# Last normalisation behind the gelus, one mask as a clamped line on ScalarE, variances by fused sums: a change to an attention and product-key kernel

## What is computed

```
q = einsum('bne', x, w_q); mean, var over all tokens
q = (q - mean) * rsqrt(var + 1e-5) * gamma + beta
sim = einsum('pbnhd,hkpd->pbnhk', q, keys)        # 2 halves x 8 heads x 32 keys
sx, ix = top_k(sim[0], 8);  sy, iy = top_k(sim[1], 8)
all_scores = sx[:, None] + sy[None, :]            # 8 x 8 per head
scores, pk = top_k(all_scores, 8)
h = gelu_new(einsum('bnd,bnhkd->bnhk', x, down_embed[indices]))
h = softmax(scores) * h
out = einsum('bnhk,bnhkd->bnd', h, up_embed[indices])
x = layernorm(x + out)
```

## Time and profile before

| | |
|---|---|
| Median of 3 runs | 651.7 us (648.76 to 651.85) |
| The profiled execution | 650.28 us, span 648.5 us |
| VectorE (DVE) busy | 541.3 us, 83% of the span |
| TensorE (PE) busy | 520.1 us, 80% |
| ScalarE (ACT) busy | 410.9 us, 63% |
| GpSimd (POOL) busy | 402.2 us, 62% |
| TensorE's granted clock | tenths 6 to 9 between the 19th and 24th of 40 slices, 9 elsewhere |

### The profile page before, as it was taken

The page is one execution under the profiler, slowest core; times in us unless marked ns, Lnnn a source line. Parts: engine busy times, 40 slices in busy tenths (PEclk is TensorE's granted clock), DMA queues, the critical chain, the costliest instruction groups (busy, mean ns, idle before and its releaser), DMA issues.

```text
span 648.5 us, 42547 instructions
## 1 busy us (share of the span) xinstructions
PE 520.1 (80%) x17953; PEld 443.2 (68%) x17985; DVE 541.3 (83%) x1741; ACT 410.9 (63%) x813; POOL 402.2 (62%) x522
## 2 busy tenths in 40 slices
PE   0279999999998899994567888887787788778776
PEld 0158878888886577784346777776776777667676
DVE  5658989889897577864788889999999999999992
ACT  4246766677775557764164576677677668667764
POOL 8345546555552235442267768878878887887882
PEclk9989999999998999996667799999999999999999
DMA  6877975654516001000012223322332332233231
GB/s 201 246 221 233 285 206 172 188 191 148 195 56 226 17 18 33 17 1 5 5 45 54 66 48 81 77 61 64 77 76 49 81 77 58 68 77 76 50 77 44
DMA packets 45201, 64.39 MB, mean 99 GB/s; under 512 B 5488, under 2 KB 37360, under 8 KB 42608
## 3 DMA queue, kind: packets, MB, share of 16 engines
q1 hardware_dynamic: 45168, 63.97, 35.7%
HBM read 36.29 MB, written 8.65 MB: 69 GB/s over the span
## 4 chain that ended last, share of the span: by engine, by line
PE 40%; issue 17%; ACT 17%; POOL 12%; DVE 9%; DMA 3%; POOLq 1%; ACTq 1%; SPq 0%; another core or an unknown queue 0%; DVEq 0%
PE ps L754 8%; PE ps L813 5%; ACT early L1070 5%; PE ps L734 4%; ACT tile_rows L1082 4%; PE ps L769 4%; PE ps L826 4%; PE ps L744 3%; ACT L1070 3%; POOL tile_rows L663 3%; PE ps L919 3%; POOL rstd L690 2%; PE ps L780 2%; DMA xT<-terms 2%; PE ps L928 2%
## 5 line engine op out<-in xcount | busy, mean ns | idle before, releaser
L919 PE MATMUL ps<-arena,hid 128*32 128x32 f32 x8192 | 79.6, 200 | 53.8 <-DVE hid L1437 46.8
L919 PEld LDWEIGHTS ps<-arena,hid 128*32 128x32 f32 x8192 | 75.7, 112 | 60.0 <-issue 31.1
L968 ACT ACTIVATE arena<-ps 128x512 f32<-128x512 f32 x128 | 69.8, 595 | 54.3 <-PE ps L754 54.1
L928 PEld LDWEIGHTS ps<-xT,downT_sb 128*128 128x128 f32 x528 | 69.0, 204 | 13.5 <-issue 12.4
L1178 DVE TENSOR_REDUCE row_max<-ps 128x8 f32<-128x768 f32 x64 | 61.0, 953 | 17.5 <-PE ps L744 17.2
L928 PE MATMUL ps<-xT,downT_sb 128*128 (+1 forms) x528 | 68.7, 287 | 1.8 <-issue 0.2
L754 PE MATMUL ps<-ident,arena 128*128 128x128 f32 x512 | 69.3, 280 | 0.0
L940 PE MATMUL ps<-up_sb,prod 128*128 128x128 f32 x512 | 65.6, 282 | 0.3 <-DVE prod L1446 0.3
L1181 DVE TENSOR_TENSOR arena<-ps,row_max 128x768 f32<-128x768 f32 x64 | 61.3, 958 | 5.1 <-DVE row_max L1178 0.2
L669 POOL TENSOR_TENSOR wq_sb<-wq_sb,tile_rows 128x1024 f32<-128x1024 f32 x32 | 64.6, 2018 | 1.0 <-POOL tile_rows L663 0.4
L940 PEld LDWEIGHTS ps<-up_sb,prod 128*128 128x128 f32 x512 | 62.9, 196 | 0.5 <-DVE prod L1446 0.5
(11 more groups left out here) (161 smaller groups left out, 1332.5 us busy)
## 6 DMA issues: line engine op xcount, KB each, us to landing
arena<-r_x SPq DMA_DIRECT2D x128, 128.0 KB, 2.4
early<-terms SPq DMA_DIRECT2D x8, 720.0 KB
xT<-terms SPq DMA_DIRECT2D x8, 720.0 KB
hid<-terms SPq DMA_DIRECT2D x8, 720.0 KB
prod<-terms SPq DMA_DIRECT2D x8, 720.0 KB
x_pair<-in_x_wrapped SPq DMA_DIRECT2D x16, 256.0 KB, 4.5
xT_tile<-xT SPq DMA_DIRECT2D x34, 64.0 KB, 1.9
x<-in_x SPq DMA_DIRECT2D x8, 256.0 KB, 2.9
```

Source lines behind the costliest of these rows:

```text
L919: mm = nc.tensor.matmul(slots[32 * g:32 * g + 32, k, c], leftT[p][:, r // 2, r % 2, :], blocks_of[p][:, :, r // 2, r % 2, GROUP * g:GROUP ...
L928: mm = nc.tensor.matmul(ps[:, 4 + half, (c % 4) * P:(c % 4 + 1) * P], downT_sb[:, c * P:(c + 1) * P], xT[:, tok(t)].rearrange("p (q r k) - ...
L968: return nc.scalar.activation(out_ap, in_ap, ACT.Copy)
```

## The change

Three edits.

The first moves work on ScalarE. In `d_act` the limits are copied ahead of the exponentials, and `last_norm` of the older tile runs behind the gelus of tile t + 1 and the table load that follows them.

The second takes the fourth left mask from VectorE. Its comparison covers three masks, 128x256x3 elements instead of 128x1024. ScalarE's new `first_keys` writes the fourth as relu(1 + 2^110 * s): s is 0 for the largest key and negative for the others. VectorE's `masks` now waits for `firsts_done` where it waited for `relexp_done`, and POOL's `classes` waits for it too. `first_keys` itself waits until the left buffer has been transposed. In VectorE's order `normaliser` moves from ahead of the right mask to behind it.

The third replaces, for the variances, each product over three heads and each sum over them by one step for each head, which multiplies and writes the sum.

```diff
--- before.py
+++ after.py
@@ -49,6 +49,7 @@
 Q_SPLIT = (slice(0, 3 * QB), slice(3 * QB, PH))
 MASKED = -1e30
 SLACK = 2.0 ** -21
+STEEP = 2.0 ** 110
 TABLES = "natural_log_exp_and_others"
 
 
@@ -281,7 +282,6 @@
         r3_done = sem("r3_done")
         moment_ready = sem("moment_ready")
         z_banks = sem("z_banks")
-        prod_done = sem("prod_done")
         q_step = sem("q_step")
         q_var_done = sem("q_var_done")
         q_rstd_done = sem("q_rstd_done")
@@ -308,6 +308,7 @@
         limits_done = sem("limits_done")
         edges_done = sem("edges_done")
         masked = sem("masked")
+        firsts_done = sem("firsts_done")
         scaled = sem("scaled")
         right_ready = sem("right_ready")
         classes_done = sem("classes_done")
@@ -672,6 +673,7 @@
             def classes(t, p):
 
                 pool.wait_ge(masked, 2 * t + 2)
+                pool.wait_ge(firsts_done, t + 1)
                 hold(pool)
                 nc.gpsimd.tensor_tensor(left[p][:, :, :, 0:TERMS - 1], left[p][:, :, :, 0:TERMS - 1],
                                         left[p][:, :, :, 1:TERMS], ALU.subtract).then_inc(classes_done, 1)
@@ -1090,6 +1092,13 @@
                 copy(limits[p][:, :, 2:5:2].rearrange("p h a -> p a h"), top_rel[:, :, 1].rearrange("p (a h) -> p a h", a=2))
                 copy(limits[p][:, :, 7:10:2], stretch(top_rel[:, 0:PK_HEADS, 1:2], 2)).then_inc(limits_set, 1)
 
+            def first_keys(t, p):
+
+                need(a, leftT_done, t - 1)
+                nc.scalar.activation(left[p][:, :, :, TERMS - 1].rearrange("p i h -> p h i"),
+                                     ps[:, p, 0:PK_HEADS * KEYS].rearrange("p (h k) -> p h k", h=PK_HEADS), ACT.Relu,
+                                     bias=1.0, scale=STEEP).then_inc(firsts_done, 1)
+
             def last_mean(t, p):
 
                 a.wait_ge(up_done, t + 1)
@@ -1123,8 +1132,9 @@
                 for p in range(2):
                     t, o = 2 * i + p, 1 - p
                     if have(t + 1):
+                        set_limits(t + 1, o)
                         rel_exps(t + 1, o)
-                        set_limits(t + 1, o)
+                        first_keys(t + 1, o)
                     if have(t - 2):
                         last_mean(t - 2, p)
                     if have(t + 1):
@@ -1132,10 +1142,11 @@
                     if have(t - 2):
                         last_square(t - 2, p)
                         last_variance(t - 2)
-                        last_norm(t - 2, p, i - 1)
                     if have(t + 1):
                         gelus(t + 1, o)
                         a.preload_act_table_set(TABLES)
+                    if have(t - 2):
+                        last_norm(t - 2, p, i - 1)
             over_tiles(a, d_act)
 
 
@@ -1319,18 +1330,15 @@
                 v.wait_ge(z_banks, b + 1)
                 z3 = ps[:, b, 0:n * (P + 1)].rearrange("p (k c) -> p k c", c=P + 1)
                 V.tensor_copy(q_mean[:, QB * b:QB * b + n], z3[:, :, P])
-                V.tensor_tensor(prod[:, QB * b:QB * b + n, :], z3[:, :, 0:P], wqT_sb[:, QB * b:QB * b + n, :], ALU.mult
-                                ).then_inc(prod_done, 1)
-
-            def q_sums(b):
-                n = min(QB, PH - QB * b)
-                v.wait_ge(prod_done, b + 1)
-                return V.tensor_reduce(q_var[:, QB * b:QB * b + n], prod[:, QB * b:QB * b + n, :], AX_X, ALU.add)
-
+                for k in range(n):
+                    last = V.scalar_tensor_tensor(prod[:, QB * b + k, :], z3[:, k, 0:P], 1.0, wqT_sb[:, QB * b + k, :], ALU.mult,
+                                                  ALU.mult, accum_out=q_var[:, QB * b + k:QB * b + k + 1])
+                return last
 
             def q_variance(part):
 
                 ks = Q_SPLIT[part]
+                v.wait_ge(q_step, 3 * part + 1)
                 V.tensor_tensor(q_mean2[:, ks], q_mean[:, ks], q_mean[:, ks], ALU.mult).then_inc(q_step, 1)
                 v.wait_ge(q_step, 3 * part + 2)
                 V.tensor_tensor(q_var[:, ks], q_var[:, ks], q_mean2[:, ks], ALU.subtract).then_inc(q_step, 1)
@@ -1352,12 +1360,11 @@
                                 ).then_inc(keys_ready, 1)
 
             for b in range(6):
-                q_moments(b)
-                if b % 3:
-                    q_sums(b - 1)
+                last = q_moments(b)
                 if b % 3 == 2:
-                    q_sums(b).then_inc(q_step, 1)
+                    last.then_inc(q_step, 1)
                     q_variance(b // 3)
+
             def split_constants(part):
 
                 cols = slice(Q_SPLIT[part].start * KEYS, Q_SPLIT[part].stop * KEYS)
@@ -1418,11 +1425,13 @@
             def masks(t, p):
 
                 sims = ps[:, p, :].rearrange("p (a h k) -> p a k h", a=2, h=PK_HEADS)
-                v.wait_ge(relexp_done, t + 1)
+                v.wait_ge(firsts_done, t + 1)
                 V.tensor_tensor(right[p], bcast(sims[:, 1], 3, TERMS), bcast(limits[p][:, :, 3:7], 1, KEYS), ALU.is_ge
                                 ).then_inc(masked, 1)
+                normaliser(t, p)
                 v.wait_ge(edges_done, t + 1)
-                V.tensor_tensor(left[p], bcast(sims[:, 0], 3, TERMS), bcast(limits[p][:, :, 0:4], 1, KEYS), ALU.is_ge
+                V.tensor_tensor(left[p][:, :, :, 0:TERMS - 1], bcast(sims[:, 0], 3, TERMS - 1),
+                                bcast(limits[p][:, :, 0:TERMS - 1], 1, KEYS), ALU.is_ge
                                 ).then_inc(masked, 1)
 
             def turn_right(t, p, i):
@@ -1461,7 +1470,6 @@
                         gate(t - 1, o)
                     if have(t + 1):
                         edges(t + 1, o)
-                        normaliser(t + 1, o)
                         masks(t + 1, o)
                     if have(t):
                         turn_left(t, p)
```

## The result

The changed kernel takes 635.1 us (median of 4 runs, 633.6 to 637.8) beside 651.8 us for the kernel before, timed with it (median of 4, 648.8 to 654.4). The ratio is 0.9768, with a 95% interval of 0.9739 to 0.9797: 15.1 us faster, between 13.2 and 17.0. The profiled execution took 636.6 us, span 634.8, which is 13.7 less than the span of the kernel before.

A forecast was written before the change was run, and what follows sets the result against it. Bound in the steady last stage: VectorE's own work beside an equally long ScalarE-POOL-VectorE ring, plus 0.21 us wait. Terms 7.0 + 0.3 + 5.5 + 0.2 = 13.0 us off 650.28 or 651.7 gave 637.8 us, range 634 to 645.

The forecast's parts named there:

- the ring: Last stage: waits circling ScalarE, POOL and VectorE, 9.4 us per tile, as long as VectorE's own work plus 0.21.
- Left mask: VectorE's left comparison, 1024 to 768 elements: 0.26 us less per tile, 7.0 us over 27 tiles.
- The ring's wait: VectorE's wait ahead of the edges (L1407), 0.21 us per tile, vanishes: 5.5 us over 26 tiles.
- The margin of 0.07 us: Edges could start at 616.82 by POOL's thresholds, while gates free VectorE at 616.89, so the wait would vanish.
- That tile: Late tile at 388.40, whose edges started 1.24 us behind the gates; taken as the distance without a wait.
- the term of 5.5 us: Gain from removing VectorE's wait ahead of the edges: 0.21 us in each of 26 tiles.
- The line's cover: ScalarE's new fourth-left-mask activation takes 0.65 us, ready 0.7 to 1.1 us before VectorE's right mask; costs nothing.
- Late reciprocal: Reciprocal behind the right mask ends about 618.6; POOL's scaling keeps its place, 0.6 us left before the next maxima.
- Query variances: Preparation: sixteen fused product-and-sum steps at 0.30 us each replace six products and six reductions; gain 0.2 us.
- the lower bound: One fused step at 0.20 us, from a 128-element product's distance to the next instruction; gain then 1.3 us.
- The rule on table loads: 1.38 us drain per ScalarE table load would need some 10.3 us per tile, making the change slower; forecast rejected it.

The follow-up runs named there:

- Cutting the ring alone: Kernel before with only the last normalisation moved behind the gelus; 0.99% faster, 6.4 us, period 9.258 us.
- the steep line's run: Kernel before with the second edit alone: fourth left mask on ScalarE, reciprocal still ahead of the right mask; 648.9 us beside 650.5, period 9.466.
- the kernel with two lines: Changed kernel with the first right mask also written by ScalarE, VectorE's right comparison covering three masks; 625.4 us, ratio 0.9614, period 8.664.
- reciprocal back: Changed kernel with the softmax's sum and reciprocal put back ahead of the right mask; 636.8 us, ratio 0.9793, period 8.998.
- exponentials first: Changed kernel with the exponentials put back ahead of the limits; 636.4 us, ratio 0.9782, period 8.996.
- line three times: Changed kernel with ScalarE's fourth-left-mask activation computed three times per tile, two into spare buffers; 635.4 us, ratio 0.9763, period 8.992.
- the fused sums: Kernel before with the third edit alone, one product-and-sum step per head; 0.51% faster, 3.3 us, ratio 0.9949.
- line five times: Changed kernel with ScalarE's fourth-left-mask activation computed five times per tile, four into spare buffers; 652.6 us, ratio 1.0039, period 9.594.
- the two with the second line: Changed kernel plus a ScalarE-written first right mask, with the reciprocal late (625.4 us) or back ahead of the right mask (626.6 us).

## Why the prediction was right

The forecast was 13.0 us of gain in the sum and 637.8 us; measured were 15.1 us (13.2 to 17.0) and 635.1, inside the range of 634 to 645. The 13.0 lies just below the measured interval. In the two profiles the last stage, for which the terms add up to 12.8, gained 12.6; the preparation, put at 0.2, gained 2.2.

- **What bounds.** Shown. VectorE's own work and the ring were 0.2 us apart. Cutting the ring alone gave a period of 9.26, shortening VectorE alone left 9.47, both together gave 8.99 (the other two moves, limits ahead of the exponentials and the late reciprocal, were worth nothing when put back). The gains do not add: 0.21 and 0.00 alone, 0.47 together. The prediction's sentence that shortening VectorE alone would be paid back at the wait is the steep line's run.
- **Left mask.** Forecast 0.26 us per tile, from 1.01 ns per element. In the steep line's own run, where the order on VectorE is the old one, the row fell from 1218 to 952 ns, 0.27, and the right mask stayed at 1240. In the changed kernel the left one is at 910 ns and the right one at 1282. That is the order, not the work: each mask's row is 0.04 shorter where it stands right behind the reciprocal (right 1241 there and 1282 elsewhere, left 910 and 952). So 0.27 net. With the ring's 0.21 this is 0.47 for each of 25 tiles, 11.85 us measured against 11.75 forecast.
- **The ring's wait.** The 0.21 us are gone, measured from the tile that the forecast took as free of waits. The margin of 0.07 us was not there, though. That tile (388.40, edges 1.24 behind) was itself still held: its edges start 0.04 us after POOL's thresholds end, and the free distance is the 1.18 of the last tile. L651 also starts 0.08 us after the classes end (603.13 to 603.21), not 0.02. So the term of 5.5 us came out by a tie within 0.04 us, which is luck in part. VectorE's gates and POOL's chain to the thresholds both follow from the same event, the last maxima of the tile, so the period does not change their distance; that is argued, and the kernel with two lines agrees (gates at 547.34, edges at 548.55, 1.21 apart).
- **The line's cover.** Forecast 0.65 us and a slack of 0.7 to 1.1; measured 0.67 and 1.37. The slack was larger since consecutive activations overlap: the exponentials occupy 0.89 of their 1.10 us (601.04 to 601.93).
- **Late reciprocal.** Forecast to leave POOL's scaling where it was; this step of the prediction is wrong. Its own numbers had the reciprocal end at 618.6, after POOL's start at 618.53, and a handover comes on top. POOL waits 0.43 us for it (605.82), and its wait ahead of the maxima is down to 0.29, where 0.6 was expected to be left; it costs nothing, as the run with the reciprocal put back shows.
- **Query variances: the term that was mis-sized.** The step in the prediction was "I take 0.30" for one fused step, with a gain of 0.2 us. A fused step takes 0.28 us, starts 0.21 after the one before, and its read of the sum, 0.08, lies beside the next step:

```profile
308.14 0.28 DVE L1334 SCALAR_TENSOR_TENSOR prod<-ps,wqT_sb 128x128 f32<-128x128 f32 x1
308.35 0.08 DVE L1334 DVE_READ_ACCUMULATOR prod<-ps,wqT_sb 128x1 f32 x1
308.35 0.28 DVE L1334 SCALAR_TENSOR_TENSOR prod<-ps,wqT_sb 128x128 f32<-128x128 f32 x1
```

So the lower bound was the right one; ScalarE's read of a sum, 0.21, was a poor guide for VectorE's. That is 1.4 us (1.55 in the changed kernel) instead of 0.2, and the rest up to 2.2 us, at the clock of the first similarities, was in nobody's sum. With 2.2 instead of 0.2 the sum would have been 15.0 instead of 13.0; that this is so near the 15.1 is chance, since the part at the clock comes in some profiles only and the first copy of means, which no edit touches, starts anywhere between 305.7 and 309.1 us.
- **The rule on table loads.** The Trainium skill (ScalarE: Activation LUTs, What ACT_TABLE_LOAD costs) adds a drain of about 1.38 us to each load. No row here has one: in the changed kernel the load at 597.21 is followed at 598.51 by the normalisation, 1.30 us later. With it ScalarE could not have kept a period of 8.66 with two lines, where it idles only 0.6 to 0.9 us per tile.

## What to carry to other kernels

When the busiest engine still shows a short regular wait, follow that wait round: if the way comes back to where it started after just one period, there are two bounds side by side. Here shortening the busy engine alone changed the period by nothing, and cutting the way round alone gained no more than the wait, 0.21 us. Move the call that waits longest (here the last step of an old tile, stuck ahead of independent work) behind that work, then shorten the busy engine, and price both together. For work moved to another engine, compare when it ends with when it is wanted, not the engine's busy share; dosing it (three times, five times) finds the end of the cover. And a wait without a bracket can still be one: compare the start of an instruction with the end of what releases it, in a tile that waits and in one that does not.

## What had not been expected

The time from the first to the seventh maxima subtraction, which holds the stretch that TensorE bounds, differs from profile to profile by more than the edits explain. Four kernels with one and the same period (8.99 to 9.00) have 57.4 (reciprocal back), 58.6 (exponentials first), 59.7 (changed) and 61.4 us (line three times). The kernel before has 60.2, with the fused sums 60.3; the others lie between 56.6 (steep line alone) and 62.6 (line five times). This one stretch spreads by 4 us among those four, more than most single edits here are worth, while the mean of the 25 tiles behind it repeats to 0.01 us.

It goes with the clock that TensorE is granted. From 345 to 386 us the mean is 0.95 to 0.99 in the four kernels with 56.6 to 57.8 us (steep line alone, reciprocal back, and the two with the second line), and 0.88 to 0.91 in the eight with 58.6 to 62.6. Whether the clock makes the stretch longer or a longer pause lowers the clock, and what sets either, was not tried.
